# Eleven expert tiles of the first batch in three fp32r passes on split weights and tokens, and the expert bias spread over four row groups

## The reference, cut to what matters

```python
x = x + xattn(layernorm(x), ctx, ctx)
x = x + attn(layernorm(x))            # also normalizes inside
# feed-forward, x normalized first
logits = x @ W_router                 # 512 x 4
expert_idx = argmax(logits)
h = gelu(einsum('th,ehi->tei', x, W1) + b1)   # W1: 4 x 512 x 2048
y = h[expert_idx] @ Wo + bo + x
x = x + layer_norm(y)
```

## Time and profile before

| | |
|---|---|
| median of three runs | 529.68 us (528.67 to 530.13) |
| profiled execution | 528.53 us |
| its span, first to last instruction | 526.8 us |
| what lies around the span | 1.73 us |
| PE busy | 509.7 us (97%) |
| DVE / ACT / POOL busy | 267.2 (51%) / 250.0 (47%) / 38.4 us (7%) |
| mean granted TensorE clock | 0.998 |

### The profile page before, as it was taken

One profiled execution on the slowest core, in us unless ns is written; L12 is line 12 of the kernel. 1 busy time (PEld: TensorE's weight loads), 2 busy tenths in 40 slices (PEclk: granted clock), 3 DMA queues, 4 the chain that ended last, 5 costly groups with the idle time before them and its releaser, 6 DMA issues.

```text
span 526.8 us, 9139 instructions
## 1 busy us (share of the span) xinstructions
PE 509.7 (97%) x3702; PEld 372.5 (71%) x3702; DVE 267.2 (51%) x562; ACT 250.0 (47%) x389; POOL 38.4 (7%) x32
## 2 busy tenths in 40 slices
PE   8999999999999999999999999898999999999994
PEld 6786776777777777988876778656675446877652
DVE  3737524546464542444485665520285537966332
ACT  4130119494948531347377577574164207755210
POOL 0220000000396000000000000000000010000000
PEclk9999999999999999999999999999999999999999
DMA  8900000000530022210400000871996975874000
GB/s 264 356 0 1 1 1 0 3 0 2 170 151 2 1 81 81 90 71 1 141 2 2 1 1 1 319 322 49 401 408 226 372 268 182 331 291 171 0 21 20
DMA packets 11745, 63.29 MB, mean 120 GB/s; under 512 B 1588, under 2 KB 2612, under 8 KB 4788
## 3 DMA queue, kind: packets, MB, share of 16 engines
q1 hardware_dynamic: 11704, 62.71, 31.7%
HBM read 62.18 MB, written 0.52 MB: 119 GB/s over the span
## 4 chain that ended last, share of the span: by engine, by line
PE 84%; ACT 8%; issue 3%; DVE 3%; DMA 1%; SPq 0%; POOLq 0%; DVEq 0%; ACTq 0%
PE ps L1010 35%; PE ps L1076 10%; PE ps L1270 10%; PE ps L1090 6%; PE ps L1064 5%; PE ps L1317 5%; ACT Pm L391 4%; PE ps L1297 3%; PE ps L1298 3%; PE ps L1299 3%; ACT PT L399 2%; PE ps L1004 1%; DMA ctx_first<-in_ctxT 1%; PE ps L1280 1%; PE ps L1195 1%
## 5 line engine op out<-in xcount | busy, mean ns | idle before, releaser
L399 ACT COPY PT<-ps 128x512 f32<-128x512 f32 x128 | 68.8, 591 | 30.5 <-PE ps L1076 30.4
L664 DVE TENSOR_SCALAR_CACHE_REDUCE Pm<-ps,small 128x512 f32<-128x512 f32 x96 | 66.4, 747 | 29.1 <-PE ps L1064 29.0
L1076 PE MATMUL ps<-ident,Pm 128*128 128x128 f32 x512 | 69.9, 277 | 3.3 <-ACT Pm L391 2.4
L1076 PEld LDWEIGHTS ps<-ident,Pm 128*128 128x128 f32 x512 | 56.4, 141 | 18.8 <-issue 12.5
L391 ACT ACTIVATE Pm<-Pm,small 128x2048 f32<-128x2048 f32 x32 | 64.3, 2010 | 7.2 <-DVE Pm L664 7.2
L1270 PE MATMUL ps<-w1raw,z 128*128 128x512 f32 x128 | 57.3, 595 | 0.7 <-DVE Pm L664 0.7
L644 DVE SCALAR_TENSOR_TENSOR KrL<-ps,small,KrH 128x512 fp32r<-128x512 f32 x32 | 23.9, 747 | 59.5 <-ACT KrH L377 59.5
L1010 PE MATMUL ps<-wvH,ctxH 128*128 128x512 f32 x124 | 50.2, 405 | 1.7 <-DVE V L653 1.0
L1010 PE MATMUL ps<-ctxH,wkH 128*128 128x512 f32 x124 | 51.4, 415 | 0.0
L1010 PE MATMUL ps<-ctxL,wkH 128*128 128x512 f32 x124 | 48.6, 392 | 0.0
L1010 PE MATMUL ps<-ctxH,wkL 128*128 128x512 f32 x124 | 48.4, 390 | 0.0
(11 more groups left out here) (169 smaller groups left out, 745.4 us busy)
## 6 DMA issues: line engine op xcount, KB each, us to landing
w1raw<-in_W SPq DMA_DIRECT2D x16, 1024.0 KB, 6.9
w2raw<-in_W SPq DMA_DIRECT2D x16, 1024.0 KB, 5.0
raw<-in_ctxT SPq DMA_DIRECT2D x7, 1024.0 KB, 5.1
woF<-in_ffn_Wo SPq DMA_DIRECT2D x4, 1024.0 KB, 11.5
wo<-in_wo SPq DMA_DIRECT2D x2, 1024.0 KB, 6.1
ctx_first<-in_ctxT SPq DMA_DIRECT2D x4, 256.0 KB, 5.4
wv_raw<-in_xWv SPq DMA_DIRECT2D x2, 512.0 KB, 6.6
wq<-in_xWq SPq DMA_DIRECT2D x1, 1024.0 KB, 11.5
```

The costliest lines, as they stand in the source:

```text
L399: act.copy(PT[:, c % 2, i, :, :].rearrange("p k t -> p (k t)"), ps[:, T_BANKS[i % 2], :]).then_inc(pt_done, 1)
L664: dve.tensor_scalar(Pm[:, i, c * CH:(c + 1) * CH], ps[:, i, :], -1.0, mx[:, p % 2, i, c - 1:c] if c else NOT_YET, ALU.mult, ALU.min, accum ...
L1076: last = pe.transpose(ps[:, T_BANKS[i % 2], j * P:(j + 1) * P], Pm[:, i, c * CH + j * P:c * CH + (j + 1) * P], ident[:])
```

## The change

Tiles of the first batch are taken in the order `FIRST`. Five of them (`WHOLE`) stay four fp32 matmuls. The other eleven go in twelve fp32r matmuls, as the second batch's do. For this DVE splits the first batch's masked tokens (`first_tokens_split`, cast 128x128 and 128x1280, and two subtractions), and every such tile is rounded once and subtracted once: tiles 4, 5, 6 both on DVE while the last pass of the cross attention runs; 8 and 9 rounded on POOL; 7, 10, 11, 12, 13, 15 rounded on ACT; all subtractions on DVE, in line with the second batch's chain. There are five load buffers and five for rounded tiles, in memory that other tensors have left, so most loads wait for another tile than before, and SP's order is written out anew. `expert_bias(0)` moves from behind the last tile to ahead of `logits(1)`, one tile (the 14th) moves from ahead of `normalized_T(1)` to behind `logits(1)`, and one from ahead of `masks(1)` to behind it. The bias is laid out so that quarter c of b1 lies on rows 32c to 32c+3; the one-hot choice is repeated 32 times before its transpose, so each quarter's product has a row group of its own. The rounding of tile 2 of the second batch waits for the end of tile 15 of the first.

```diff
+        FIRST = (0, 1, 4, 5, 6, 2, 3, 7, 8, 9, 10, 11, 12, 13, 14, 15)
+        WHOLE = (0, 1, 2, 3, 14)
+        w1_kb = (64, 72, 80, 88, 56)
+        RAW_OF = {0: 0, 1: 1, 4: 2, 5: 3, 6: 0, 7: 1, 2: 2, 3: 3, 8: 4, 9: 0, 10: 2, 11: 3, 12: 1, 13: 4, 14: 0, 15: 2}
+        HIGH_OF = {4: "C", 5: "A", 6: "B", 7: "D", 8: "A", 9: "C", 10: "E", 11: "B", 12: "D", 13: "A", 15: "B"}
+        b1raw = at("b1raw", [P, CH], F32, 160)
-        b1raw = at("b1raw", [E, I], F32, 160)
...
+            sp.wait_ge(qkv_mm[1], 3)
+            first_in_(8)
+            for t, freed in ((9, 6), (10, 2), (11, 3), (12, 7)):
+                sp.wait_ge(first_tile, USED[freed])
+                first_in_(t)
+            sp.wait_ge(pv2_mm, 2)
+            second_in(0)
+            sp.wait_ge(first_tile, USED[8])
+            first_in_(13)
+            second_in(1)
+            sp.wait_ge(first_tile, USED[9])
+            first_in_(14)
...
+            sp.wait_ge(first_tile, USED[10])
+            first_in_(15)
...
+            first_high(7, None)
             transposed(yT[1], yT_mm, 1, SPARE, yT_done)
...
             values2(1)
-            act.wait_ge(b1_in, 16)
-            act.copy(b1H[:], b1raw[:]).then_inc(b1_hi, 1)
+            first_high(10, None)
+            first_high(11, 6)
             outputs2_T(1)
+            first_high(12, 7)
+            first_high(13, 8)
+            first_high(15, 11)
             transposed(yT[1], x2T_mm, 1, XT_BANKS[1], x2T_done)
             transposed(yTH, x2T_mm, 1, XT_BANKS[1], yT_hi)
+            second_high(0)
             masks(1)
...
+            def first_halves(t):
+                pe.wait_ge(first_split, 2 + SPLIT.index(t) + 1)
+                for c in range(IC):
+                    pe.matmul(ps[:, c, :], zH_, wH[:, cc], start=False, stop=False)
+                    pe.matmul(ps[:, c, :], zH_, wL[:, cc], start=False, stop=False)
+                    last = pe.matmul(ps[:, c, :], zL_, wH[:, cc], start=False, stop=(t == FIRST[-1]))
             def expert_bias(b):
-                for c in range(IC):
-                    for part in (b1H, b1L):
-                        last = pe.matmul(ps[:, 4 * b + c, :], ohT[b][:], part[:, c * CH:(c + 1) * CH], start=False,
+                for part in (b1H, b1L):
+                    for c in range(IC):
+                        r = slice(DH * c, DH * c + E)
+                        pe.matmul(ps[:, 4 * b + c, :], ohT[b][r, :], part[r, :], start=False, stop=False)
```

More of the change, by code:

```diff
@@ L200, in perceiver_block @@
         qkv1_in = [sem(f"qkv1_in{k}") for k in range(3)]
-        w1_in = [sem(f"w1_in{i}") for i in range(RING)]
+        w1_in = [sem(f"w1_in{i}") for i in range(len(w1_kb))]
+        first_hi_pool, first_hi_act, first_split = (sem(n) for n in ("first_hi_pool", "first_hi_act", "first_split"))
         w2_in = [sem(f"w2_in{i}") for i in range(RING2)]
@@ L313, in _ @@
-            for n in range(2, NW1):
-                w2_tile_in(n)
+            sp.wait_ge(first_tile, USED[10])
+            first_in_(15)
+            sp.wait_ge(first_tile, USED[11])
+            second_in(2)
+            sp.wait_ge(first_tile, USED[12])
+            second_in(3)
+            ffn_wo_in(2)
+            ffn_wo_in(3)
+            sp.wait_ge(first_tile, USED[14])
+            second_in(4)
+            sp.wait_ge(w1_mm[0], IC)
+            second_in(5)
+            for n in range(RING2, NW1):
+                sp.wait_ge(w1_tile, n - RING2 + 1)
+                second_in(n)
@@ L568, in _, with first_high, second_high @@
             reciprocals_T(NP - 1)
+            def first_high(t, freed):
+                if freed is not None:
+                    act.wait_ge(first_tile, USED[freed])
+                act.wait_ge(w1_in[RAW_OF[t]], LOADED[t])
+                act.copy(w1H[HIGH_OF[t]][:], w1raw[RAW_OF[t]][:]).then_inc(first_hi_act, 1)
+            def second_high(n):
+                act.wait_ge(w2_in[n % RING2], 16 * (n // RING2 + 1))
+                if n == 0:
+                    act.wait_ge(cT_dve[1], 2 * HPG)
+                elif n == 1:
+                    act.wait_ge(o2_mm, 2)
+                elif n == 2:
+                    act.wait_ge(w1_mm[0], IC)
+                else:
+                    act.wait_ge(w1_tile, n - 2)
+                act.copy(w2H[n % 3][:], w2raw[n % RING2][:]).then_inc(w1_hi, 1)
+            act.wait_ge(b1_in, 16)
+            act.copy(b1H[:], b1raw[:]).then_inc(b1_hi, 1)
+            act.wait_ge(wo_mm, 2)
+            first_high(7, None)
             transposed(yT[1], yT_mm, 1, SPARE, yT_done)
@@ L1277, in expert_bias @@
                 pe.wait_ge(ohT_ready, b + 1)
-                for c in range(IC):
-                    for part in (b1H, b1L):
-                        last = pe.matmul(ps[:, 4 * b + c, :], ohT[b][:], part[:, c * CH:(c + 1) * CH], start=False,
-                                         stop=(b == 0 and part is b1L))
-                    if b == 0:
-                        last.then_inc(w1_mm[b], 1)
+                for part in (b1H, b1L):
+                    for c in range(IC):
+                        r = slice(DH * c, DH * c + E)
+                        pe.matmul(ps[:, 4 * b + c, :], ohT[b][r, :], part[r, :], start=False, stop=False)
             def second_experts(n):
@@ L1414, in _ @@
             attention2_out(1)
-            for n in range(11, 14):
+            for n in range(11, 13):
                 first_experts(n)
             normalized_T(1)
+            expert_bias(0)
             logits(1)
-            first_experts(14)
+            first_experts(13)
             masks(1)
             onehots_T(1)
+            first_experts(14)
             first_experts(15)
-            expert_bias(0)
             for n in range(NW1):
@@ L1467 @@
         "rows": np.stack([v[n] for n in ROWS]),
-        "W_router": tiles(v["L0_ffn_W_router"]), "W1": v["L0_ffn_W1"], "b1": v["L0_ffn_b1"],
+        "W_router": tiles(v["L0_ffn_W_router"]), "W1": v["L0_ffn_W1"],
+        "b1": np.tile(v["L0_ffn_b1"].reshape(-1, 4, CH).transpose(1, 0, 2), (1, 8, 1)).reshape(P, CH),
         "ffn_Wo": tiles(v["L0_ffn_Wo"]),
```

186 lines of the change are left out of this document (123 added, 63 removed).

## The result

The changed kernel took 525.75 us (median of 4, 525.27 to 525.96), beside 529.9 us (528.67 to 531.2) for the kernel before on the same chip: ratio 0.9917, 95% interval 0.99 to 0.9935. That is faster, but by 4.15 us where 8.6 was forecast, and 525.75 lies above the range. The profiled execution took 525.27 us, with a span of 523.5.

The account below looks back on a forecast made before the run. PE, busy 97% of the span, was taken as the bound. A shift of -7.9 us by the second batch's start, +0.8 wait and -1.47 bias gave -8.6: median 529.68 to 521.1 us, range 519.3 to 524.6.

Parts of the forecast that it names:

- The ceiling from PE's work: PE: eleven tiles save 0.71 us each, 7.8, and two biases 1.47 each; 10.7 us in all before waits.
- the price taken from the scores step: Each bias on PE: two overlapping fours of matmuls and a start gap, 0.57 us instead of 2.04.
- rival C: Bias matmuls on row groups of 4 rows don't overlap on PE; 523.4 us, chance 0.07.
- The wait ahead of `tokens_T(1)`: PE waits 0.6 us before the first batch's token transposes at about 374.5, losing most of tile 5's 0.71 saving.
- The one ahead of `normalized_T(1)`: PE waits 1.2 us before the transposes at 422.8 for DVE's normalized tokens.
- The wait at tile 5 of the second batch: PE waits 0.8 us, once, for DVE's split of that tile.
- the bound I had used: DVE's casts of tiles 4 to 6 cost at most a subtraction, 2.29 us each; no cost to the end.
- four signs: Wrong if: split-tile wait over 1 us, tile 15's cast ending after 424, bias matmuls 0.23 us apart, reciprocal after 405.5.
- I take 0; up to +1.5: Tile 15's load lands about 421, its cast on ACT ends about 423, before the transposed tokens due at 423.4.
- I take 0, as the cast ends at 396.0: POOL's cast of tile 9 ends before DVE's shuffle of V at 396.1; no cost, at the other end +1.5 us.
- B: DVE's split chain runs late and delays the attention chain; 522.3 to 525.5 us, middle 523.7, chance 0.25.
- E: Slower: tile 15's load, landing at about 430, holds ACT's transposed tokens; 530 us, chance 0.04.

Follow-up runs that it names:

- e4: Changed kernel with the fourth expert's masks of the second batch after DVE's subtraction of tile 6 instead of tile 4; 524.7 us.
- f4: Changed kernel with SP issuing tile 15's load ahead of the second batch's tile 1 and the three loads of rows; 521.09 us.
- e1: Changed kernel with ACT's cast of tile 15 behind the two copies of the transposed tokens instead of ahead of them; 522.21 us.
- g1: Changed kernel with nine unread fp32 identity matmuls on PE between the first batch's bias and logits; 523.79 us.
- e3: e1 with POOL's cast of tile 9 waiting until DVE's shuffle of V is done; 522.51 us.
- f1: e1 with the masks of e4 and tile 9 cast on ACT between softmax exponentials instead of on POOL; 518.82 us.
- g2: f1 with tile 15's load issued early as in f4; 519.14 us.
- f2: f1 with three identity matmuls on PE in the wait ahead of the last token transposes; 518.75 us.

## Why the prediction was wrong in size

**What held.** The ceiling from PE's work: tiles 8, 9 and 10 went from 404.59 to 412.89, 2.77 us each with the start of the line, and PE's busy time fell by 7.3 us with more instructions. The bias on four row groups: two fours 0.34 us apart in the first batch; in the second 0.33, and 0.67 until the next instruction, so the price taken from the scores step, 0.57, was 0.1 too low, and rival C was out. The wait ahead of `tokens_T(1)`: 0.46, forecast 0.6. The one ahead of `normalized_T(1)`: 0.88, forecast 1.2. The wait at tile 5 of the second batch: 1.08, forecast 0.8, in its place and by its cause (e4). DVE's casts of tiles 4 to 6 went faster than the bound I had used, with no effect on the end.

Of the four signs that I had named, three came: PE waited 1.08 us at a split tile, the cast of tile 15 ended at 425.96, and the reciprocal started just past 405.5 in before's time. The bias matmuls did overlap.

**Step that failed first: "I take 0; up to +1.5" for tile 15's load.** I had named the place and its chain, and then priced it by a landing at about 421, from 4.75 MB at 424 GB/s. Measured, the load landed at 424.06 (424.7 in before's time). Part of it is arithmetic: tile 12's load, issued at 402.81, was also ahead of it (ahead of that the queue was empty: a window from 402.9 to 403.7 has 0 GB/s). Part is rate: 397 GB/s from 412 on, against the 424 I used. And part is order. In the two long windows above, 8 us x 353 GB/s + 12.06 us x 397 GB/s is 7.6 million bytes moved from 404 on, while all that was issued from tile 12's load to tile 15's own is 6.75 MB, 7.1 million bytes. At least 0.5 million of it belonged to loads that SP issued later, from 419.24 on. The Trainium skill, "DMA: Bandwidth & Descriptors", section "Queues, rings and completion order", says that data descriptors carry no barrier, so that a later one may finish its write before an earlier one. The bytes here agree with it, though they don't tell whether that happened within one DMA engine or by one engine running ahead of another. The wait that came out is 2.45 us instead of none; f4 and e1 show that it was this load and this order on ACT.

**Step that was missing: the clock.** The sum had PE's waits as lost time only. Nowhere did it ask what an idle stretch does to the work after it. Measured, 2.35 us on the way to the second batch; g1 gets it back (13.37 to 10.93 us from the logits on) with the wait still there. The Trainium skill, "TensorE: Matmul & The Clock Gate", section "HAM oscillation — how this bites in real kernels", describes it: a kernel that waits on a DMA between bursts of matmuls starts the next burst at the lower clock. This trace agrees, with 0.50 from 426 to 431; that the clock fell only 0.9 us into the wait, and in e1 with PE at work, shows that the long wait is not the whole condition. I had not used the page, as the trace of before shows only 1.00 there. The two errors aren't independent: the second happened because the first did, and that made 4.7 us out of a place that I had given at most 1.5.

**Step that failed third: "I take 0, as the cast ends at 396.0" for POOL.** The cast ended at 396.66, 397.3 in before's time and so 1.3 us late, since tile 9's load had held POOL for 1.80 us; DVE's shuffle behind it ended at 397.68. The cost is 1.0 us on the shuffle and 0.7 to 0.85 on the path. With e3's cast at 4.03 us the runs show the exclusion from both sides: whoever comes second stands for nearly all that is left of the other's instruction. The rule of the Trainium skill, "SBUF — State Buffer", section "Who interferes with whom", that I had weighed against the earlier trace rows was right. The row was a poor witness, as that step had met only the cast's last 0.31 us; it also ended 0.2 us sooner than if it had stood still from its start (0.31 + 0.29 against 0.39). The shuffle did so by 0.14 and e3's cast by 0.12, so some 0.1 to 0.2 us at the start of the second instruction seem not to be held. DVE's softmax steps, which read PSUM, kept their 0.69 us beside POOL's casts, as I had assumed.

**The end.** From the second batch's first tile on, 83.54 us instead of 83.76; forecast was a gain of 0.67. The missing 0.45 is 0.28 at tile 5, 0.1 at the bias, and less than 0.1 that I can't place.

**Of the rivals**, B had the direction (delays handed to the attention chain) but by load and POOL, not by an overfull DVE, and its range ended at 525.5. E was the right mechanism at the right place, and I had given it 0.04 since I only worked out when it would eat the whole gain. It wanted a price for a landing some microseconds late, and got none.

**What stays open.** What decides the clock at the margin. With the wait gone it still fell for 3.4 us in e1's profiled execution and not in those of e3, which has the same order on ACT, or of f1 to f4 and g2, and mean clocks of single executions go from 0.993 to 0.999 for f1 (520.12 and 518.75 us). A mean clock says so only roughly, since it also takes in a fall behind PE's last work, which costs nothing (f2's profiled execution has 0.997 from such a fall alone, at about 513 us). None of the runs tells why one execution of the same program keeps it.

## What to carry to other kernels

When a term of the sum is "up to 1.5, taken as 0", ask first what is queued behind that wait on its engine, and take an instruction that waits for a load out from ahead of one that the critical chain needs: the move of one line on ACT was worth 3.5 us. Price an idle stretch of PE twice, once as waiting and once as the work that may follow at half clock; a fill of useless matmuls in the wait is a cheap experiment to tell the two apart. And when POOL shares a tile's work with DVE, moving it to another moment only moved the cost here (e3), as DVE was busy in SBUF there too; ACT had the room for it (f1).

## What the runs showed of the hardware

The scatter of the kernel before is a scatter of its clock too: its executions with a mean granted clock of 0.998 took 528.4 to 528.7 us, those with 0.994 or 0.995 took 529.4 to 530.7, those at 0.990 to 0.992 took 529.8 to 531.6. The 1.15 us by which I raised the forecast, median above profiled execution, was therefore probably also a fall of the clock: 0.003 of 527 us is 1.6 (an estimate; the clocks of those three executions are not known). An fp32 matmul of 128x128 is two instructions of PE, 0.24 us together. And DVE's cast of a 128x2048 tile from fp32 to fp32r takes 1.22 us where ACT takes 1.90 and POOL 1.89.
